# A six-layer attention and mixture-of-experts kernel: expert sum in three steps, ordered attention products, shorter elu, normalisation on ScalarE, new order lists

## What is computed

```python
x = x + 0.5 * _L0_ffn_ref(_layernorm(x), ...)    # MOE0_A
x = x + _L0_attn_ref(_layernorm(x), ...)         # ATT0
x = x + 0.5 * _L0_ffn_ref(_layernorm(x), ...)    # MOE0_B
x = x + 0.5 * _L1_ffn_ref(_layernorm(x), ...)    # MOE1_A
x = x + _L1_attn_ref(_layernorm(x), ...)         # ATT1
x = x + 0.5 * _L1_ffn_ref(_layernorm(x), ...)    # MOE1_B
```

```python
y = relu(einsum('nh,edh->ned', flat, expert_w) + expert_b)
out = sum over the two chosen experts of y * weight
```

## Time and profile before

| | |
|---|---|
| median of three runs | 790.63 us (790.29 to 792.37) |
| the profiled execution | 791.16 us, span 789.4 us |
| granted TensorE clock, mean | 0.929 |
| PE busy | 687.4 us (87%) |
| DVE busy | 605.3 us (77%) |
| ACT busy | 405.8 us (51%) |
| Pool busy | 87.8 us (11%) |
| DVE sums over experts (L696) | 75.6 + 44.7 us, x32 |
| Pool outer products (L370) | 34.2 us, x16 |

### The profile page before, as it was taken

One profiled execution on the slowest core, in us unless ns is written; L12 is line 12 of the kernel. 1 busy time (PEld: TensorE's weight loads), 2 busy tenths in 40 slices (PEclk: granted clock), 3 DMA queues, 4 the chain that ended last, 5 costly groups with the idle time before them and its releaser, 6 DMA issues. The chain is left out here.

```text
span 789.4 us, 7776 instructions
## 1 busy us (share of the span) xinstructions
PE 687.4 (87%) x2522; PEld 455.5 (58%) x2522; DVE 605.3 (77%) x1138; ACT 405.8 (51%) x801; POOL 87.8 (11%) x68
## 2 busy tenths in 40 slices
PE   3599999998999999999999898999999976476754
PEld 2455565654656766666666655657666464364543
DVE  4687588557545975987699969887958679969968
ACT  4253565646546665436776464557566335224324
POOL 2120020000100013100101131001000030022000
PEclk9889999998999999999999999989999979658768
DMA  8642542071333223422120042200523000000000
GB/s 237 178 86 64 86 76 54 19 134 42 77 54 53 56 53 83 73 60 54 53 54 0 1 98 56 64 0 1 108 55 80 1 0 1 0 1 0 0 15 14
DMA packets 26952, 42.25 MB, mean 54 GB/s; under 512 B 1627, under 2 KB 8860, under 8 KB 26908
## 3 DMA queue, kind: packets, MB, share of 16 engines
q1 hardware_dynamic: 26910, 41.74, 24.3%
HBM read 40.43 MB, written 1.31 MB: 53 GB/s over the span
## 5 line engine op out<-in xcount | busy, mean ns | idle before, releaser
L516 ACT ACTIVATE g<-ph,b1col 128x512 f32<-128x512 f32 x256 | 171.7, 691 | 162.1 <-PE ph L805 118.9
L1006 PE MATMUL py<-hw,w2s 128*128 128x512 f32 x512 | 249.5, 611 | 4.9 <-DVE hw L763 4.8
L763 DVE TENSOR_TENSOR hw<-g,bc 128x1024 f32<-128x1024 f32 x128 | 162.4, 1279 | 78.7 <-ACT g L516 58.9
L803 PE MATMUL ph<-xbh,w1h 128*128 128x512 f32 x256 | 140.0, 547 | 6.1 <-DVE xbl L601 4.3
L1006 PEld LDWEIGHTS py<-hw,w2s 128*128 128x128 f32 x512 | 96.5, 193 | 80.5 <-issue 63.7
L804 PE MATMUL ph<-xbl,w1h 128*128 128x512 f32 x256 | 103.3, 404 | 0.0
L805 PE MATMUL ph<-xbh,w1l 128*128 128x512 f32 x256 | 103.2, 403 | 0.0
L349 POOL TENSOR_TENSOR rstd<-vare,mhalf 128x4 f32<-128x4 f32 x24 | 34.4, 1432 | 579.3 <-DVE vare L591 579.3
L472 ACT ACTIVATE stage<-ps,comb 128x128 f32<-128x128 f32 x240 | 64.9, 393 | 26.5 <-PE ps L928 26.2
L696 DVE TENSOR_REDUCE red<-stage 128x128 f32<-128x2048 f32 x20 | 75.6, 3778 | 2.2 <-issue 0.4
L803 PEld LDWEIGHTS ph<-xbh,w1h 128*128 128x128 f32 x256 | 50.2, 196 | 40.3 <-issue 28.1
(11 more groups left out here) (166 smaller groups left out, 990.0 us busy)
## 6 DMA issues: line engine op xcount, KB each, us to landing
bc<-comb_rows SPq DMA_DIRECT2D x32, 1024.0 KB, 8.7
stage<-in_L_ffn_W_dram SPq DMA_DIRECT2D x4, 512.0 KB, 6.6
X<-in_L_attn_x_dram SPq DMA_DIRECT2D x4, 256.0 KB, 3.2
out_dram<-X SPq DMA_DIRECT2D x4, 256.0 KB, 5.5
comb_rows<-combT SPq DMA_DIRECT2D x8, 32.0 KB, 2.2
side<-in_L_attn_wq_dram SPq DMA_DIRECT2D x1, 64.0 KB
side<-in_L_attn_wk_dram SPq DMA_DIRECT2D x1, 64.0 KB
side<-in_L_attn_wv_dram SPq DMA_DIRECT2D x1, 64.0 KB
```

Of the source, the lines that this page charges most:

```text
L516: nc.scalar.activation(g[:, s % 2, h, :], ph[:, (HC * s + h) % RING_PH, :], ACT.Gelu, bias=b1col[:, HC * e + h:HC * e + h + 1]).then_inc(g ...
L763: V.tensor_tensor(hw[:, s % RING_HW, :, :], g[:, s % 2, :, :], bc[:, s // GQ % 2, s % GQ, :].unsqueeze(1).to_broadcast([P, HC, CH]), ALU.m ...
L803: T.matmul(dst, wh, xh, start=True, stop=False)
L1006: ins = T.matmul(py[:, :], w2s[:, w], hw[:, s2 % RING_HW, h, :], start=e2 == 0 and h == 0, stop=False)
```

## The change

The sum over 16 experts becomes: Pool adds halves (1024 elements), Pool adds quarters (512), DVE reduces four (512 elements read in order). For this the relu outputs are laid out as (group, feature, expert of the group), so neighbouring features are 16 bytes apart when written. In `a1` the outer product, the product with q and the sum over d use (head, e, d) order, so that d is innermost. elu+1 is `min(exp(x), 1) + relu(x)` in one DVE operation; exp reads PSUM. `xn` is made on ACT as `rstd*x + (-mean*rstd)`; DVE makes `-mean`, Pool the product `nmr`. On DVE the wait for `comb` moves from the start of `f1` to its first relu. The order lists of all engines are replaced, with the same stages in LIGHT, HEAVY and LATE in the same order. Slices are written by a table PIECES, of which the entries used are the four chunks as before; widths and counts stay the same. SP's list is unchanged in effect.

```diff
             def ln(l, c):            # Pool
                 pool.wait_ge(light["stat"], nth_light("stat", l, c))
-                nc.gpsimd.tensor_tensor(rstd[:, :], vare[:, :], mhalf[:, :], ALU.pow).then_inc(light["rstd"], 1)
+                n = ntiles(c)
+                nc.gpsimd.tensor_tensor(rstd[:, 0:n], vare[:, 0:n], mhalf[:, 0:n], ALU.pow).then_inc(light["rstd"], 1)
+                pool.wait_ge(light["rstd"], nth_light("rstd", l, c))
+                nc.gpsimd.tensor_tensor(nmr[:, 0:n], nmean[:, 0:n], rstd[:, 0:n], ALU.mult).then_inc(light["nmr"], 1)
...
-                    kb = qk[:, t, P:2 * P].rearrange("p (h d) -> p h d", d=HD).unsqueeze(3).to_broadcast([P, HEADS, HD, HD])
-                    vb = v1[:, t, :].rearrange("p (h e) -> p h e", e=HD).unsqueeze(2).to_broadcast([P, HEADS, HD, HD])
+                    kb = qk[:, t, P:2 * P].rearrange("p (h d) -> p h d", d=HD).unsqueeze(2).to_broadcast([P, HEADS, HD, HD])
+                    vb = v1[:, t, :].rearrange("p (h e) -> p h e", e=HD).unsqueeze(3).to_broadcast([P, HEADS, HD, HD])
...
+            def f1_(l, c):           # Pool
+                late, signal, n = moe1(l, c)
+                r = rel_late if late else rel
+                for j in range(ntiles(c)):
+                    pool.wait_ge(signal["relu_a"], (n + j + 1) * ACT_GROUPS)
+                    pool.wait_ge(signal["relu_v"], (n + j + 1) * (GROUPS - ACT_GROUPS))
+                    lo, hi = (r[:, j % 2, a * E * D // 2:(a + 1) * E * D // 2] for a in range(2))
+                    nc.gpsimd.tensor_tensor(lo, lo, hi, ALU.add).then_inc(signal["half"], 1)
+                    pool.wait_ge(signal["half"], n + j + 1)
+                    l4, h4 = (lo.rearrange("p (a n) -> p a n", a=2)[:, a, :] for a in range(2))
+                    nc.gpsimd.tensor_tensor(l4, l4, h4, ALU.add).then_inc(signal["quarter"], 1)
+                    yield
...
             def ln(l, c):            # ACT
-                yield
+                act.wait_ge(light["nmr"], nth_light("nmr", l, c))
+                for j in range(ntiles(c)):
+                    ins = nc.scalar.activation(xn[:, j * D:(j + 1) * D], X[:, tile_(c, j)], ACT.Identity,
+                                               bias=nmr[:, j:j + 1], scale=rstd[:, j:j + 1])
+                ins.then_inc(light["xn"], 1)
...
-                                ins = nc.scalar.activation(r[:, j % 2, e * D:(e + 1) * D], banks[:, u % 3, i * D:(i + 1) * D], ACT.Relu,
-                                                           scale=comb[:, c, j, e:e + 1])
+                                ins = nc.scalar.activation(r[:, j % 2, :].rearrange("p (a d e) -> p d a e", a=4, d=D)[:, :, e // 4, e % 4], banks[:, u % 3, i * D:(i + 1) * D], ACT.Relu,
+                                                           scale=comb[:, PIECES[c][0] + j, e:e + 1])
...
+                nc.scalar.activation(qk_r[:, 0:n, :], qk_ps, ACT.Relu).then_inc(a1["relu"], 1)
+                nc.scalar.activation(qk_m[:, 0:n, :], qk_ps, ACT.Exp).then_inc(a1["exp"], 1)
...
             def ln(l, c):            # DVE
+                V.tensor_scalar(nmean[:, 0:n], mv[:, 0:n, 0], -1.0, None, ALU.mult)
...
-                    (klink if late else hlink)(V.tensor_reduce(sum_[:, :], r[:, j % 2, :].rearrange("p (e d) -> p d e", e=E), AX, ALU.add))
+                    dve.wait_ge(signal["quarter"], n + j + 1)
...
+                    (klink if late else hlink)(V.tensor_reduce(sum_[:, :], r[:, j % 2, 0:E * D // 4].rearrange("p (d e) -> p d e", d=D), AX, ALU.add))
...
-                V.tensor_scalar(qk_m, qk_ps, 0.0, None, ALU.min).then_inc(a1["min"], 1)
...
-                hlink(V.scalar_tensor_tensor(qk_r, qk_m, -1.0, qk_r, ALU.add, ALU.add))
-                V.tensor_scalar(qk[:, :, :], qk_r, 1.0, None, ALU.add).then_inc(a1["qk"], 1)
+                V.scalar_tensor_tensor(qk[:, 0:n, :], qk_m[:, 0:n, :], 1.0, qk_r[:, 0:n, :], ALU.min, ALU.add).then_inc(a1["qk"], 1)
```

More of the change, by code:

```diff
@@ L3, with drive @@
 from contextlib import ExitStack
+TURNS = {
[18 rows of a table added]
+}
+def drive(engine, streams):
+    for turn in TURNS[engine].split():
+        for _ in range(int(turn[1:] or 1)):
+            next(streams[turn[0]])
+    for stream in streams.values():
+        assert next(stream, "end") == "end"
 def build_program(nc, x, wq, bq, wk, bk, wv, bv, wo, bo, Wr, br, W1, b1, W2, b2,
@@ L86, in build_program @@
         vare = sb("vare", [P, TPC])
-        rstd = sb("rstd", [P, TPC])
+        rstd, nmean, nmr = (sb(n, [P, TPC]) for n in ("rstd", "nmean", "nmr"))
         xn = sb("xn", [P, TPC * D])
@@ L164, in build_program @@
                                           "vz", "o_ps", "o", "x")}
-        f1 = {(l, late): {n: sem(f"f{l}_{late}_{n}") for n in ("y_ps", "relu_a", "relu_v", "red")}
+        f1 = {(l, late): {n: sem(f"f{l}_{late}_{n}") for n in ("y_ps", "relu_a", "relu_v", "half", "quarter", "red")}
               for l in (MOE1_A, MOE1_B) for late in (0, 1)}
-        a1 = {n: sem("a1_" + n) for n in ("qk_ps", "v_ps", "relu", "v", "min", "exp", "qk", "x", "kv", "kvh", "kvl", "kc_ps",
+        a1 = {n: sem("a1_" + n) for n in ("qk_ps", "v_ps", "relu", "v", "exp", "qk", "x", "kv", "kvh", "kvl", "kc_ps",
                                           "cum_ps", "prod", "att", "at_ps", "at", "o_ps")}
@@ L242, in moe1, with nth_a1, tiles_a1, streams @@
             before = [t for t in (LATE if late else HEAVY) if t[0] in ("f1", "g1") and t[1] == l]
-            return late, f1[l, late], before.index(("g1" if late else "f1", l, c))
+            return late, f1[l, late], sum(ntiles(t[2]) for t in before[:before.index(("g1" if late else "f1", l, c))])
         def summed(l, c):
             _, signal, n = moe1(l, c)
-            return signal["red"], TPC * (n + 1)
-        def drive(turns, main, stages):
+            return signal["red"], n + ntiles(c)
+        def nth_a1(c):
+            return [t[2] for t in HEAVY if t[0] == "a1"].index(c)
+        def tiles_a1(c):
+            return sum(ntiles(t[2]) for t in HEAVY[:HEAVY.index(("a1", ATT1, c))] if t[0] == "a1")
+        def streams(main, stages):
             def halves():
@@ L261, in steps @@
                     yield from stages[s](l, c)
-            streams = {"m": halves(), "l": steps(LIGHT), "h": steps(HEAVY), "k": steps(LATE)}
-            for turn in turns.split():
-                for _ in range(int(turn[1:] or 1)):
-                    next(streams[turn[0]])
-            for stream in streams.values():
-                assert next(stream, "end") == "end"
+            return {"m": halves(), "l": steps(LIGHT), "h": steps(HEAVY), "k": steps(LATE)}
         def tile_(c, j):
-            return slice(c * CH + j * P, c * CH + (j + 1) * P)
+            return slice((PIECES[c][0] + j) * P, (PIECES[c][0] + j + 1) * P)
         def w1_part(i):
@@ L323, in _ @@
                         sp.dma_start(be_raw[r:r + 1, :], expert_b.rearrange("(a e) d -> a (e d)", a=1)).then_inc(w_in["be"], 16)
-            for c in range(NCH):
+            last = [t[2] for t in LIGHT if t[0] == "ln" and t[1] == MOE1_B]
+            for c in last:
                 sp.wait_ge(*summed(MOE1_B, c))
-                sp.dma_start(out_t[:, TPC * c:TPC * (c + 1), :], X[:, col(c)].rearrange("p (t d) -> p t d", d=D)).then_inc(stored, 16)
-            sp.wait_ge(stored, 16 * NCH)
+                sp.dma_start(out_t[:, tiles(c), :], X[:, col(c)].rearrange("p (t d) -> p t d", d=D)).then_inc(stored, 16)
+            sp.wait_ge(stored, 16 * len(last))
         @block.gpsimd
@@ L379, in a1_ @@
                 yield
-                for t in range(TPC):
+                for t in range(n):
                     yield
-                    if 2 <= t + 1 < TPC:
+                    if 2 <= t + 1 < n:
                         outer(t + 1)
@@ L495, in a1_ @@
                 yield
-                for t in range(TPC):
+                for t in range(n):
                     yield
-                    if t + 1 < TPC:
+                    if t + 1 < n:
                         high(t + 1)
@@ L856, in rt @@
                     pe.wait_ge(w_in["router"], 32)
+                n = ntiles(c)
                 if moe0(l):
-                    T.matmul(pl[:, 0:TPC * 2 * E], ones[0:1, :], brr.rearrange("p t a e -> p (t a e)"), start=True, stop=False)
+                    T.matmul(pl[:, 0:n * 2 * E], ones[0:1, :], brr[:, 0:n, :, :].rearrange("p t a e -> p (t a e)"), start=True, stop=False)
                 w = wr0 if moe0(l) else wr1
-                for j in range(TPC):
+                for j in range(n):
                     t = slice(j * P, (j + 1) * P)
@@ L863, in rt @@
                     T.matmul(d, hi[:, t], w[:, :], start=not moe0(l), stop=False)
-                    ins = T.matmul(d[:, 0:E], lo[:, t], w[:, 0:E], start=False, stop=j == TPC - 1 or not moe0(l))
+                    ins = T.matmul(d[:, 0:E], lo[:, t], w[:, 0:E], start=False, stop=j == n - 1 or not moe0(l))
                 ins.then_inc(light["lg_ps"], 1)
```

(4 more changed lines are left out.)

303 lines of the change are left out of this document (152 added, 151 removed), and 33 rows, old and new, of tables (TURNS, TURNS_ACT, TURNS_DVE, TURNS_PE).

## The result

The changed kernel takes 800.25 us (median of 4 runs, 798.09 to 801.84) against 790.5 for the kernel before beside it: ratio 1.0108, 95% interval 1.0077 to 1.014. The forecast was 745, range 722 to 775, so a gain of 46 us was expected and 10 us were lost. The profiled execution has a span of 796.4 us.

A forecast was written before the change was run, and what follows sets the result against it. PE was taken to bound the main phase and DVE's queue the tail. Main phase -10, tail parts -18, -10 and -5 make -43; less 3 for Pool's pipeline, plus 6 for clock: -46, so 791.2 to 745 us, range 722 to 775.

The forecast's parts named there:

- Pool's adds as parallel work: Late expert tiles: ACT, Pool and DVE overlap over two buffer halves, 3.9 us per tile against 4.87 before.
- Part C: Tail from chunk 3's attention add to the last X add, 37.0 us before: 5 us less.
- main phase -10: Stretch up to the last c0 add: 8 us of PE's idle time come back and 2 of clock; bounds 0 and -25.
- The prediction's own sign of being wrong: Main phase ending later than before would mean that the new order, not the sums, decides.
- zero for the order lists: All engines' lists: stages interleaved a few positions apart cost nothing, covered by PE's saturation; bound -5 to +10.
- Part A: Tail from the last c0 add to chunk 2's attention add: 43 to 47 us instead of 63.6, -18.
- Part B: Tail from chunk 2's attention add to chunk 3's: 42 us instead of 52.4, -10.
- the clock's 6 us: Tail: a denser PE is granted a higher clock for about 85 us of its work, gaining 6 us.
- the operations that DVE loses: DVE: expert reduce 0.69 us for 3.78, attention reduce 1.22 for 2.09, elu's min (1.22) and +1 (0.69) gone.
- rival 4: Twelve relus of each tile: ACT's strided writes cost 49 us, less 25 saved elsewhere; 810 to 820 us, chance 0.09.
- the small ones: Pool's 1024-element add 1.96 us, its 512-element add 1.27, `xn` on ACT 0.27 each, Pool's `nmr` 0.3.
- Rival 2: Tail: Pool takes DVE's place, its adds lengthened by collisions to 5.1 us per tile; +30, 770 to 780 us, chance 0.21.

The follow-up runs named there:

- old_dve3: The kernel before plus ordered attention products, short elu and the three-step expert sum, all on DVE; 764.42 us, ratio 0.9641.
- pool_late: old_dve3 with the sum's first two adds on Pool in the twelve late tiles only; 785.93 us, ratio 0.9942.
- pool_main: old_dve3 with the sum's first two adds on Pool only in the twenty tiles beside the slots; 791.48 us, ratio 1.0022.
- new_dve3: old_dve3 with the new order lists; 787.46 us, ratio 0.9935.
- DVE3: The expert sum in three steps, all on DVE, as in old_dve3 (764.42 us) and new_dve3 (787.46 us).
- old_order_norm_dve: The changed kernel with normalisation back on DVE and the order of before for PE, ACT and DVE; Pool keeps its new list; 813.03 us, ratio 1.0259.
- norm_dve: The changed kernel with its new order lists, only the normalisation back on DVE; 798.47 us, ratio 1.0080.
- old_dve3_xn_act: old_dve3 with the normalisation `xn` on ACT and its product `nmr` on Pool; 796.09 us, ratio 1.0071.

## Why the prediction was wrong, step by step

- **Failed first: Pool's adds as parallel work.** The late tile was computed as a two-buffer loop, 3.9 us, with ACT, Pool and DVE overlapping. It is 5.9: the sum overlooked DVE's own relu (1.05), which stands behind DVE's wait and ahead of Pool's next add, so that DVE and Pool take turns. From the first relus to the last X add the last four tiles take 26.3 us (767.28 to 793.60) where the sum had 20.0. The first comes out as forecast, after 8.7 us; the other three follow 5.9 us apart. The question "what is queued behind the waiting instruction" was asked of Pool and not of DVE. With the adds on DVE a late tile takes 4.07 us, in old_dve3. Shown by the timeline, by pool_late, pool_main and the waits. Part C was to fall by 5 and rose by 2.
- **Failed: main phase -10.** It was +25. The prediction took DVE's freed busy time as PE's gain, 8 us of PE's idle time back and 2 of clock. The path splits it: in old_dve3 the c0 mark is 626.2, 7.5 us ahead of before (the forecast's sign, nearly its size, but from a smaller saving on DVE; PE's idle time between 60 and 600 us did fall by 8.2); Pool's adds bring it to 653.0, the new lists leave it there (653.2), the normalisation on ACT makes it 658.7. The prediction's own sign of being wrong, a later end of the main phase, came, but its reading, "the new order, and not the sums", holds only in part: with the order of before Pool's adds alone bring 653.0, the new lists alone (new_dve3) 641.0.
- **Failed: zero for the order lists** (bound -5 to +10). They are worth +31, +23 or -14, by what they are combined with. "PE's saturation" was no cover: with DVE3 the new lists move the c0 mark from 626.2 to 641.0. The +31 and +23 are in both halves, the -14 is all in the tail. Which engine's list does it was not tried, and by what mechanism stays open.
- **Part A held in number**, 45.6 for 43 to 47, and partly by luck. With the order of before the same sums and Pool's adds give 61.4 us for it (old_order_norm_dve), under the new lists 49.2 (norm_dve); so the lists, priced at nothing, bring 12 of the 18 us, and at a mark that lies 25 us later. Part B was 50.3 for 42, with two late tiles in it where three or four were forecast. `kvl` takes 1.64 us there and elsewhere in the mean against 1.25 in old_dve3_xn_act; but it takes 1.57 in new_dve3 too, which has no adds on Pool, so this comes with the new lists and Pool's outer products. What else ate DVE's saving in B was not measured.
- **Mis-sized or unshown: the clock's 6 us.** The granted clock in the three parts is 0.87, 0.78 and 0.73 against 0.80, 0.75 and 0.73 in about the same parts before. PE's 30.8 and 36.6 us of work in A and B would give back some 4 us at most, an estimate from these rows, and no run shows what of it reaches the end.
- **Held: the operations that DVE loses.** Reduce 0.69, attention reduce 1.22, elu 1.22 once; the strided write on ACT nearly nothing (twelve relus 3.33 to 3.43 instead of 3.20 us), rival 4 therefore out. DVE's busy time fell to 483.5 us where 465 was forecast, Pool's rose to 226.5 for 200. DVE's own relu was mis-sized, 1.05 for 0.69, within the bound given.
- **Mis-sized: the small ones.** Pool's add 2.4 alone for 1.96 (taken from L370, a multiply of broadcast operands) and 2.54 in the mean; `xn` on ACT 1.64 per four, 0.41 each for 0.27; `nmr` 0.33 for 0.3. The power has a median of 1.91 us where it was 1.03 in the earlier trace rows, but that overstates it: 15 of 24 are long where 11 were, and the mean is 1.58 against 1.43. In each long one a DVE operation with two SBUF inputs (`hw`, `qk` or `kvl`) had begun 0.17 us earlier.

```profile
L356 POOL TENSOR_TENSOR rstd<-vare,mhalf x24: 1006/1912/1925, 5.9 to 756.3; 128x4 f32<-128x4 f32 x24
```

- **The rivals.** Rival 2 had Pool take DVE's place. Two of its signs came (adds of 2.5 us, DVE idle on the second add for 57.7 us), the third, X adds over 1 us, hardly did: the twelve late ones take 0.29, the twenty others 0.39 in the mean (the longest 1.35). It priced collisions, +30, and not the round trip, and so stayed on the fast side at 770 to 780. The slower rival named ACT's writes, the wrong mechanism. One reading was off as well: during PE's wait of 8.06 us DVE is in two expert sums, not three, and then in its statistics. The Trainium skill (GPSIMD Engine Reference, "Engine selection") says that an elementwise add of two inputs is about twice as slow on GPSIMD as on VectorE; the rows agree (2.40 against 1.23 us, 1.29 against 0.69). So an add given to Pool gains only if DVE's list has other work between giving it and taking it back; here it had none for the 3.7 us.

The best version measured is old_dve3, with or without the strided layout: 764.42 and 763.17 us, 3.6% and 3.5% faster than before. Its late tile of 4.07 us is DVE's own work again (1.05+1.23+0.69+0.69+0.29 = 3.95).

## What to carry to other kernels

An engine that stands in its list for work it gave away, as DVE here, gains nothing by giving it. Moving an operation off a busy in-order engine pays only if what follows it in the list doesn't need the result, so compare the round trip (here 3.9 us) with doing it in place (1.95), not with zero. First make the operation itself cheaper where it is: three contiguous steps on the same engine (1.23+0.69+0.69) instead of one strided reduce (3.78) gained 14.6 us here, and moving two of them away lost that and more. A list and a set of operations are to be timed crosswise, the old list with the new operations too: the lists here were worth from +31 to -14 us by the operations under them.

## What was not expected of the hardware

- A DVE write in steps of 16 bytes costs about as a read in steps of 512 bytes does: 1.05 against 0.68 us for 512 elements, the reduce 1.03 against 0.68. ACT's twelve relus of 128 lose 0.1 to 0.2 us in all, so little of it shows there.
- Pool's add of 1024 elements takes 2.40 us, its multiply of as many with both operands broadcast 1.95 (L381; L370 in the earlier trace rows). Whether the operation or the operands make the difference was not tried.
- A Pool operation on 4 elements per partition, the power, takes 1.01 or 1.91 us; beside each of the fifteen longer ones in the changed kernel runs a DVE operation of 1.2 us with two SBUF inputs that had begun 0.17 us before.
